# Attention and a gated feed-forward block on one core: weight flags cut into seven groups, and the first tile's rows taken two by two

## The reference

```python
x = x + attention(layernorm(x), ctx, ctx, mask)      # scores / sqrt(256), causal, softmax, times ctx
h = silu(tlin(n, w1, s1)) * tlin(n, w2, s2)          # n = layernorm(x), 256 -> 1024
h = gelu(tlin(h, h1, sh1), approximate=False)        # 1024 -> 1024
h = gelu(tlin(h, h2, sh2), approximate=False)        # 1024 -> 1024
x = x + tlin(h, w3, s3)                              # 1024 -> 256;  tlin(x, w, s) = (x @ w.T) * s
```

## Time and profile before

| | |
|---|---|
| median of three runs | 363.35 us (361.88 to 363.49) |
| time of the profiled execution | 363.38 us |
| span of its trace | 361.6 us |
| PE busy | 354.7 us, 98% of the span |
| DVE, ACT, POOL busy | 186.5, 147.2, 37.7 us |
| products of the hidden layers (line 1046) | 400.6 us summed over overlapping records |
| first product of the feed-forward block starts | 16.16 us |

### The profile page before, as it was taken

The page is one execution under the profiler, slowest core; times in us unless marked ns, Lnnn a source line. Parts: engine busy times, 40 slices in busy tenths (PEclk is TensorE's granted clock), DMA queues, the critical chain, the costliest instruction groups (busy, mean ns, idle before and its releaser), DMA issues.

```text
span 361.6 us, 4633 instructions
## 1 busy us (share of the span) xinstructions
PE 354.7 (98%) x1738; PEld 299.5 (83%) x1738; DVE 186.5 (52%) x423; ACT 147.2 (41%) x247; POOL 37.7 (10%) x77
## 2 busy tenths in 40 slices
PE   8999998999999999999999999999999999999996
PEld 7887786887898888888898888888889888888886
DVE  4869327445657654338355845335626662323233
ACT  5888853861146623511143641621123652212120
POOL 7660103000100320001000050001000000000000
PEclk9999999999999999999999999999999999999999
DMA  8898999959277010300833010130411000000001
GB/s 269 278 469 330 379 328 380 433 135 360 66 200 295 3 29 0 79 10 21 191 117 110 2 29 0 29 60 0 101 17 56 6 0 0 2 0 0 2 0 62
DMA packets 39569, 43.82 MB, mean 121 GB/s; under 512 B 23746, under 2 KB 32068, under 8 KB 39364
## 3 DMA queue, kind: packets, MB, share of 16 engines
q1 hardware_dynamic: 38672, 42.62, 35.2%
q10 hardware_dynamic: 868, 0.80, 1.1%
HBM read 38.55 MB, written 16.39 MB: 152 GB/s over the span
## 4 chain that ended last, share of the span: by engine, by line
PE 97%; DVE 1%; issue 1%; POOL 1%; ACT 0%; DVEq 0%; POOLq 0%
PE ring L1046 65%; PE ring L1020 16%; PE ring L1065 8%; PE att L980 2%; PE att L992 2%; PE ring L1154 1%; PE ring L1200 0%; POOL weights L440 0%; PE att L1181 0%; PE ring L1181 0%; PE ring L1163 0%; ACT act L573 0%; PE att L1208 0%; POOL rstd L405 0%; DVE x_attn L783 0%
## 5 line engine op out<-in xcount | busy, mean ns | idle before, releaser
L1046 PE MATMUL ring<-h_hi,weights 128*128 128x512 f32 x512 | 201.0, 393 | 2.3 <-ACT act L573 1.5
L1046 PE MATMUL ring<-h_lo,weights 128*128 128x512 f32 x512 | 199.6, 390 | 0.0
L1046 PEld LDWEIGHTS ring<-h_hi,weights 128*128 128x128 f32 x512 | 96.2, 188 | 23.8 <-ACT act L573 1.9
L1046 PEld LDWEIGHTS ring<-h_lo,weights 128*128 128x128 f32 x512 | 96.2, 188 | 19.8
L573 ACT ACTIVATE act<-ring,scales 128x512 f32<-128x512 f32 x64 | 44.0, 688 | 154.6 <-PE ring L1046 154.6
L860 DVE CAST h_hi<-act 128x512 fp32r<-128x512 f32 x64 | 27.6, 431 | 117.8 <-ACT act L573 117.7
L726 DVE TENSOR_TENSOR h_lo<-act,h_hi 128x512 fp32r<-128x512 f32 x96 | 66.5, 692 | 2.3
L1020 PE MATMUL ring<-xn_hi,weights 128*128 128x512 f32 (+1 forms) x140 | 51.5, 374 | 0.2 <-POOL weights L440 0.2
L1020 PE MATMUL ring<-xn_lo,weights 128*128 128x512 f32 (+1 forms) x140 | 51.1, 372 | 0.0
L553 ACT ACTIVATE gate<-ring,scales 128x512 f32<-128x512 f32 x32 | 22.0, 689 | 27.1 <-PE ring L1020 27.1
L1065 PE MATMUL ring<-weights,h_lo 128*128 128x256 f32 x128 | 30.9, 284 | 0.0
(11 more groups left out here) (130 smaller groups left out, 217.7 us busy)
## 6 DMA issues: line engine op xcount, KB each, us to landing
weights<-weights_staged SPq DMA_DIRECT2D x11, 1024.0 KB, 8.7
x_in<-in_x SPq DMA_DIRECT2D x8, 256.0 KB, 4.6
ctx_cols<-in_ctx_cols SPq DMA_DIRECT2D x8, 256.0 KB, 5.6
ctx_rows<-in_ctx_rows SPq DMA_DIRECT2D x4, 512.0 KB, 7.2
out_dram<-residual SPq DMA_DIRECT2D x16, 128.0 KB, 2.1
turned<-in_x_cols SPq DMA_DIRECT2D x3, 512.0 KB, 8.7
xn_blocks<-work SPq DMA_DIRECT2D x3, 512.0 KB, 3.2
turned<-xn_blocks SPq DMA_DIRECT2D x12, 128.0 KB, 3.0
```

The lines of the kernel that those rows point to most:

```text
L1046: ins = nc.tensor.matmul(bank[:], w, part[:, k].bitcast(dt), start=(k == 0 and part is h_hi[src]), stop=(k == HC - 1 and part is h_lo[src]))
```

## The change

**Seven flags.** The ends of the groups become 2, 4, 6, 8, 12, 16, 22. `HID1B` is pieces 6, 7 (chunks 2, 3 of layer 0), `HID1C` pieces 8 to 11 (chunks 4 to 7 and the scores of tile 1), the new `HID2A` pieces 12 to 15 (chunks 0 to 3 of layer 1). ACT's tests of pieces 8 to 21 are put behind other chunks, DVE takes `HID1C` ahead of chunk 2 and `HID2A` ahead of chunk 7 of layer 0.

**The reload.** The staging of pieces 0 to 3 is issued behind `place_probs(1)`, the way of tile 1's probabilities through DRAM.

**The start.** All four engines' lists are written in another order, the rows 0 and 1 ahead of 2 and 3, with other numbers of fillers.

```diff
-GATE_UP_A, GATE_UP_B, HID1A, HID1B, HID1C, LAST = range(6)
-FLAG_ENDS = (2, 4, 6, 10, 16, PIECES)
+GATE_UP_A, GATE_UP_B, HID1A, HID1B, HID1C, HID2A, LAST = range(7)
+FLAG_ENDS = (2, 4, 6, 8, 12, 16, PIECES)
...
                 load_pieces(n)
-                if at + ahead < len(order):
+                if at + ahead < len(order) - RAW // 2 or n == 0:
                     stage(order[at + ahead])
                 if n == PIECES - 2:
                     place_probs(1)
+                    stage(0)
+                    stage(2)
...
-            tests = {"first layer": list(range(GU_P, 10))}
-            after = ((0, 0), (0, 1), (0, 2), (0, 2), (0, 3), (0, 3), (0, 6), (0, 6), (1, 0), (1, 0), (1, 1), (1, 1))
-            for n, at in zip(range(10, PIECES), after, strict=True):
+            tests = {"first layer": list(range(GU_P, 8))}
+            after = ((0, 0), (0, 0), (0, 1), (0, 1), (0, 3), (0, 3), (0, 5), (0, 5), (0, 7), (0, 7), (1, 0), (1, 0),
+                     (1, 1), (1, 1))
+            for n, at in zip(range(8, PIECES), after, strict=True):
...
-                        for flag, step in ((HID1B, (0, 0)), (HID1C, (0, 4)), (LAST, (1, 2))):
+                        for flag, step in ((HID1B, (0, 0)), (HID1C, (0, 2)), (HID2A, (0, 7)), (LAST, (1, 2))):
...
                     first_turn_xn(2)
-                    stay_busy(2)
-                    first_turn_xn(3)
                     pe.wait_ge(first_copied, QUARTERS * 2)
                     gate_and_up(0, (2,), dt, 0)
+                    first_turn_xn(3)
...
-                hid1(HID1B, *range(2, 6))
-                segment(HID1C, across_layers)
+                hid1(HID1B, 2, 3)
+                segment(HID1C, to_scores)
+                segment(HID2A, lambda dt: hidden(0, 1, range(0, 4), dt))
...
-            stay_busy(18)
+            stay_busy(13)
             pe.wait_ge(ident_made, 1)
             pe.wait_ge(first_consts, 3)
+            first_mask_in(0)
+            stay_busy(1)
             first_turn(0)
-            first_mask_in(0)
             first_turn(1)
```

More of the change, by code:

```diff
@@ L343, in _ @@
                     place_probs(1)
-                if n == FLAG_PIECES[HID1C][1] - 2:
+                    stage(0)
+                    stage(2)
+                if n == FLAG_PIECES[HID2A][1] - 2:
                     sp.wait_ge(hid_mm, RAW - GU_P)
@@ L348, in _ @@
                     load_mask(1)
-                if n == FLAG_PIECES[HID1C][1]:
+                if n == FLAG_PIECES[HID2A][1]:
                     load_values(1)
@@ L602, in _ @@
             first_queries(0)
-            first_deviation(2)
             first_queries(1)
+            first_exponentials(0)
             first_queries(2)
-            first_exponentials(0)
             first_exponentials(1)
+            first_evacuate_probs(1)
             first_exponentials(2)
-            first_evacuate_probs(1)
             first_evacuate_probs(2)
-            first_exponentials(3)
             test_piece(0)
-            first_evacuate_probs(3)
             test_piece(1)
             first_split(0)
+            first_exponentials(3)
             first_split(1)
+            first_evacuate_probs(3)
             test_piece(2)
-            test_piece(3)
             first_split(2)
             first_split(3)
+            test_piece(3)
             load_table(1, ACT.Silu)
             act.wait_ge(scales_in, 16)
-            tests = {"first layer": list(range(GU_P, 10))}
-            after = ((0, 0), (0, 1), (0, 2), (0, 2), (0, 3), (0, 3), (0, 6), (0, 6), (1, 0), (1, 0), (1, 1), (1, 1))
-            for n, at in zip(range(10, PIECES), after, strict=True):
+            tests = {"first layer": list(range(GU_P, 8))}
+            after = ((0, 0), (0, 0), (0, 1), (0, 1), (0, 3), (0, 3), (0, 5), (0, 5), (0, 7), (0, 7), (1, 0), (1, 0),
+                     (1, 1), (1, 1))
+            for n, at in zip(range(8, PIECES), after, strict=True):
                 tests.setdefault(at, []).append(n)
@@ L929, in _ @@
             first_moments_of(3, 0)
+            first_deviation(2)
             first_deviation(3)
@@ L932, in _ @@
             first_neg_max(0)
-            first_queries(3)
             first_max(1)
             first_neg_max(1)
+            first_queries(3)
             first_evacuate_probs(0)
@@ L939, in _ @@
             first_inverse(0)
-            first_max(3)
-            first_neg_max(3)
             first_attention(0)
@@ L947, in _ @@
             first_moments_of(1, 1)
+            first_max(3)
+            first_neg_max(3)
+            first_normalise(0)
+            first_normalise(1)
+            first_split(0)
+            take_summed_flag(GATE_UP_A)
+            first_split(1)
             first_inverse(1)
-            first_normalise(0)
             first_attention(2)
-            first_normalise(1)
             first_attention_stats(2)
-            take_summed_flag(GATE_UP_A)
             first_moments_of(2, 1)
-            first_split(0)
-            first_split(1)
             first_attention(3)
@@ L1115, in first_tile, with to_scores @@
                 hid1(HID1A, 0, 1)
-                hid1(HID1B, *range(2, 6))
-                segment(HID1C, across_layers)
+                hid1(HID1B, 2, 3)
+                segment(HID1C, to_scores)
+                segment(HID2A, lambda dt: hidden(0, 1, range(0, 4), dt))
                 segment(LAST, all_tested)
-            def across_layers(dt):
-                hidden(0, 0, (6, 7), dt)
+            def to_scores(dt):
+                hidden(0, 0, range(4, HC), dt)
                 scores(1)
-                hidden(0, 1, range(0, 4), dt)
             def all_tested(dt):
@@ L1212, in _ @@
             pe.wait_ge(idle_made, 1)
-            stay_busy(18)
+            stay_busy(13)
             pe.wait_ge(ident_made, 1)
             pe.wait_ge(first_consts, 3)
+            first_mask_in(0)
+            stay_busy(1)
             first_turn(0)
-            first_mask_in(0)
             first_turn(1)
             first_score(0)
+            first_score(1)
             first_turn(2)
             first_turn(3)
-            first_score(1)
+            first_turn_probs(0)
             first_mask_in(1)
-            first_turn_probs(0)
             first_score(2)
-            first_score(3)
             first_turn_probs(1)
@@ L1229, in _ @@
             first_attend(0)
+            first_attend(1)
+            first_score(3)
             first_turn_probs(2)
-            first_attend(1)
+            stay_busy(2)
             first_attend(2)
-            first_turn_probs(3)
-            stay_busy(9)
+            stay_busy(6)
             first_turn_xn(0)
-            stay_busy(2)
+            stay_busy(1)
             pe.wait_ge(ones_made, 1)
@@ L1240, in _ @@
             first_turn_xn(1)
+            first_turn_probs(3)
+            stay_busy(2)
             first_attend(3)
```

## The result

The changed kernel is slower. Six runs on one chip took 368.65 to 372.69 us, median 370.58; the kernel before took 361.88 to 363.49 beside them, median 363.19. The ratio is 1.0226, with a 95% interval from 1.0199 to 1.0253. The forecast was 364.1 and the range ended at 366.3: both missed. The profiled execution took 369.92 us, its span is 368.1. All medians here take every run of a kernel, also those well above its fastest (two of four of "reload only", two of ten of "before, 13 fillers").

What follows compares the result with a forecast made beforehand. PE's stream was taken to bound the kernel, with 97% of the chain. From 363.38 us, start +2.7, flags -2.0 and reload 0 gave 364.1 us; the eight-in-ten range was 361.0 to 366.3.

Steps and rivals of the forecast that it cites:

- What bounds the kernel: Whole kernel: PE holds 97% of the chain; the change can act only ahead of chunk 3 and at the flags.
- Flags: PE's switches at HID1B, HID1C and LAST: 2.76 us lost now, 0.75 still lost after regrouping, a gain of 2.0 us.
- 0.75 us kept back for four switches: Ready-flag switches behind chunk 7 of the gate: 0.15 us for each of three and 0.3 for LAST.
- Rival C: PE's switches: each costs what LAST costs, so the gain is only 0.16 and the time 365.9 us; chance 0.15.
- LAST's jump: PE's switch to LAST: its 0.65 us loss comes from jump distance; with a shorter jump 0.3 was taken.
- The reload: Staging of pieces 0 to 3 behind tile 1's probabilities: costs 0 us, bounds 0 and +2.
- The start: New engine lists ahead of chunk 3: first product 1.45 us later, chunk 3 later by 2.7, bounds -1.0 to +4.0.
- Test 3 ahead of the gate: ACT's list ahead of chunk 3: test 3 delays the gate, putting chunk 3 at 25.85 against PE's own 25.03.
- Rival B: PE's start: the hole after fewer fillers delays the clock's rise, adding 2.2 us, 366.3 us in all; chance 0.09.
- Rival A: Start of the kernel: the new order works, keeping -0.5 us for 360.9, or nothing for 361.4; chance 0.23.
- Rival D: Tile 1's start: the reload delays its rows' way through DRAM, about 1.5 us more, 365.6 us; chance 0.06.
- The sum: Whole kernel: 363.38 + 2.7 - 2.0 + 0 = 364.1 us, range 361.0 to 366.3.

Runs made afterwards that it cites:

- reload only: Kernel before with only the staging of pieces 0 to 3 moved behind tile 1's probabilities; 370.87 us, ratio 1.0243.
- before, 13 fillers: Kernel before with 13 fillers at the start in place of 18, nothing else; 363.79 us, ratio 1.0029.
- the flags alone: Kernel before with the seven flag groups, their tests and DVE's flags, start and reload as before; 361.47 us, ratio 0.9970.
- old reload: Changed kernel with the staging of pieces 0 to 3 back at its old places; 365.90 us, ratio 1.0087.
- held back: Kernel before with only the stagings moved, and SP held ahead of them until PE is past LAST; 369.39 us, ratio 1.0198.
- 16 fillers: Changed kernel with 16 fillers at the start in place of 13; 365.48 us, ratio 1.0084.
- 18 fillers: Changed kernel with the staging back at its old places and 18 fillers at the start; 365.55 us, ratio 1.0058.
- start only: Kernel before with only the new lists of all four engines and the fillers at the start; 365.49 us, ratio 1.0091.
- reload padded: Kernel before with only the stagings moved, and 12 fillers in place of 9 ahead of first_turn_xn(0); 368.92 us, ratio 1.0169.

## Why the prediction was wrong, point by point

- **What bounds the kernel**: right. PE holds 95% of the chain after, and all differences lie ahead of chunk 3 and at the flags.
- **Flags, -2.0 (bounds -2.76 to -0.16)**: right in mechanism and size in the profiles, -2.32 in the changed kernel and -2.85 with the flags alone. In the medians it is -1.2; the wait at HID1C is absent in four other profiles with the old groups, so it was in part luck of the execution that I read. From chunk 3 to `attend` the flags alone take 59.83 us where 62.80 were taken before, 2.97 less: a little beyond the bound of 2.76. The 0.75 us kept back for four switches was too much: all four cost 0 there. Rival C, each switch at LAST's price, fell.
- **LAST's jump.** The prediction took its 0.65 us for a matter of how far PE jumps, and gave 0.3. The distance did shrink and the hole grew to 3.43. The Trainium skill, "Runtime: NRT & Kernel Launch", section "Instruction fetch mechanics", says that a taken branch out of the pages at hand needs a DMA before PE can go on. By that rule, the traces agree that a fetch stands ahead of the hole; but the rule was used for whether there is a fetch, and what counted was what else is on the DMA engines while it is under way.
- **The reload, 0 (bounds 0 and +2)**: this is the step that failed, by 4.53 us in the profile and 4.7 in the medians. I asked who waits for the data of the moved stagings, and found slack at tile 1 and at the probabilities; both were right (tile 1's first product stands unbroken behind `down`). I did not ask who else uses the DMA engines at the new place. The earlier trace rows was also misread: not "90% busy or more until 90.4", but 80% or more with one slice of 50% to 60%, from 72.3 to 81.4. That slice looks like room, and the stagings moved into it; what they met there, by the reading of the fetches above, was not the kernel's own traffic. The 0.49 us at LAST, ended by "issue" with its flag ready for 2 us, was the sign: something outside the semaphores was late there already. In its place the runs show a hole of 3.43 us and a lower clock behind it, which come with the moved stagings (reload only) and go when they are put back (old reload) or held back; the queueing of PE's fetch is the reading that fits, not a proof. With 16 fillers the same stagings cost nothing at LAST, so the term depends on when the fetch falls.
- **The start, +2.7 (bounds -1.0 to +4.0)**: right in sign, mechanism and order of waits. With the early clock it is +3.0 to +3.2 (26.12 to 26.36 against 23.13), 0.3 to 0.5 over the forecast. Test 3 ahead of the gate was in the sum at 0.82 (25.85 less 25.03) and measured 0.44. One term was too short: the first product came 2.2 us later (18.32) where 1.45 was forecast. With 16 fillers row 1's exponentials start at 8.87 (8.2 forecast), test 0 at 13.00 (12.2), and row 3's copy ends at 17.11 (16.25): nearly all of it arises ahead of the tests. (The durations listed behind the tests add up to 1.94; the sum uses 1.6, and 1.72 was measured.)
- **Rival B, the clock, given 0.09 at +2.2**: it came true beside the rest. The scores' records of 2.46 to 2.90 us in place of 1.55 are the double lengths that it named, and chunk 3 comes 1.3 to 2.4 us later with it. With the new order the clock records reach the higher level at 8.83 to 10.72 in five profiled executions of eight and at 4.90 to 5.51 in three; with the old order at 4.04 to 5.91 in all six. That PE has more idle places at the new start is in the rows, but neither 18 fillers in the new order nor 13 in the old one decides it, so the cause is not settled.
- **Rival A** fell: the start keeps nothing. **Rival D** did not occur in the changed kernel, and occurs when the stagings are held back (4.93 us).
- **The sum** after the fact: +4.50 - 2.32 + 4.53 = +6.71 in the profile. The range ended 4.3 us too low, since the bounds of the reload came only from waits for its data.

## What to carry to other kernels

A DMA that nobody waits for can still cost: before large transfers are moved, look at what an engine fetches at the same time, above all at a branch, and suspect an exposed transfer behind an idle time ended by "issue" with a ready flag. Here the holes of 3.43 to 5.98 us were paid a second time in lower clock, 1.3 to 1.5 times their length in all; the one of 1.56 was not. Read a wait that depends on a DMA's landing from more than one execution before its removal is booked as a gain, and where a change has independent parts, take the part that pays: the flags alone gave 361.47 us, against 370.58 for all.

## What was not expected of the hardware

- A fetch of 16 KB of instructions near LAST took 1.0 to 1.65 us under the kernel's own transfers, and where PE stood it resumed 2.20 to 2.29 us after its end. The stall at one jump was 0 to 5.98 us with the same distance jumped (start only; reload padded).
- Standing still for 3.43, 3.65, 5.98 and 4.93 us was followed each time by products at 0.42 us or more in place of 0.23, with a granted clock between 0.50 and 0.64 over the next stretch of 4 us; standing still for 1.56 us was not.
- At the start, programs that differ in a few fillers met the higher clock early or late: the scores of two rows took 1.55 us in three of the profiled executions with the new order and 2.46 to 2.90 in five. The Trainium skill, "TensorE: Matmul & The Clock Gate", section "What's actually happening", says that the lower level is the default and activity lifts it. By that rule one expects the rise in every execution, and the traces agree: it comes in all 14, between 4.04 and 10.72 us. What sets its moment no run here shows.
- The ready-flag switches cost nothing that the trace can tell: 128 products over two of them in 29.30 us, and none lost at the third, 69.18.
